# Attention in a perceiver block: the output stage one tile later, evacuations dealt out anew, input transposes between the value products

## The reference, cut to what matters

```python
# x: (32, 64, 128), ctx: (32, 128, 128), 16 heads of width 8
q = (layernorm(x) @ Wq + bq)        # 32 x 64 queries
k, v = ctx @ Wk + bk, ctx @ Wv + bv # 32 x 128 keys, values
scores = where(keep, q @ k.T / sqrt(8), neg)     # per batch row and head
out = softmax(scores) @ v
x = x + out @ Wo + bo               # stage 1, attention: the change is here
x = x + scan_block(layernorm(x))    # stage 2, a linear scan
for router in routers:              # stage 3, four layers, one expert of 16 per token
    xt = xt + w * (silu(xt @ W1[e]) @ W2[e])
```

## Time and profile before

| what | value |
|---|---|
| median of three runs | 614.9 us (609.98 to 617.53) |
| the profiled execution | 620.82 us, span of the core 619.1 us |
| TensorE busy in the span | 496.2 us (80%), granted clock 0.942 on average |
| VectorE busy | 333.5 us (54%) |
| ScalarE busy | 274.6 us (44%) |
| GpSimd busy | 197.0 us (32%) |
| chain that ended last, by engine | PE 56%, DVE 18%, issue 8%, DMA 6%, ACT 4% |

### The profile page before, as it was taken

The page is one execution under the profiler, slowest core; times in us unless marked ns, Lnnn a source line. Parts: engine busy times, 40 slices in busy tenths (PEclk is TensorE's granted clock), DMA queues, the critical chain, the costliest instruction groups (busy, mean ns, idle before and its releaser), DMA issues.

```text
span 619.1 us, 16857 instructions
## 1 busy us (share of the span) xinstructions
PE 496.2 (80%) x5788; PEld 403.8 (65%) x5788; DVE 333.5 (54%) x746; ACT 274.6 (44%) x684; POOL 197.0 (32%) x243
## 2 busy tenths in 40 slices
PE   2586868686777877799976799977799987599894
PEld 1365656575554633799943799943599963399792
DVE  3466666665664769345528445527544534744442
ACT  1455555565455430565510466620366621166440
POOL 7233131312001114433532532531541550541343
PEclk9799999998988987999999799997799997899988
DMA  5100000049200020110120110030110112010005
GB/s 134 32 17 19 12 20 12 18 150 328 81 3 2 1 68 8 35 28 19 37 85 1 39 32 15 36 94 0 31 34 9 40 42 58 22 31 19 24 31 152
DMA packets 30690, 28.11 MB, mean 45 GB/s; under 512 B 4624, under 2 KB 24464, under 8 KB 30608
## 3 DMA queue, kind: packets, MB, share of 16 engines
q1 hardware_dynamic: 26512, 18.62, 10.3%
q0 software_dynamic: 4096, 8.40, 4.4%
HBM read 20.71 MB, written 6.29 MB: 44 GB/s over the span
## 4 chain that ended last, share of the span: by engine, by line
PE 56%; DVE 18%; issue 8%; DMA 6%; ACT 4%; POOL 4%; another core or an unknown queue 1%; SPq 1%; DVEq 0%; POOLq 0%; ACTq 0%
PE bank L787 17%; PE bank L800 16%; PE bank L637 5%; DVE ppT L896 3%; PE bank L618 3%; PE bank L599 3%; DMA cur<-token_rows 3%; DVE rden L902 3%; DVE ohr L1065 2%; PE bank L593 2%; DMA ppT<-token_rows,token_i 1%; DMA token_rows<-ysort,token_i 1%; POOL token_rows L390 1%; PE bank L776 1%
## 5 line engine op out<-in xcount | busy, mean ns | idle before, releaser
L1114 DVE SCALAR_TENSOR_TENSOR pp<-pp,bank 128x512 f32<-128x512 f32 x124 | 85.4, 688 | 129.7 <-ACT pp L539 127.0
L800 PE MATMUL bank<-w,pp 128*128 x992 | 137.2, 282 | 12.7 <-DVE pp L1114 10.6
L787 PE MATMUL bank<-vm,ppT 128*128 x992 | 138.3, 285 | 0.0
L800 PEld LDWEIGHTS bank<-w,pp 128*128 128x128 f32 x992 | 123.1, 195 | 15.8 <-issue 15.3
L787 PEld LDWEIGHTS bank<-vm,ppT 128*128 128x128 f32 x992 | 126.2, 199 | 1.3 <-issue 0.2
L539 ACT ACTIVATE pp<-bank 128x512 f32<-128x512 f32 x124 | 74.2, 598 | 101.0 <-PE bank L787 87.6
L530 ACT COPY ppT<-w 128x512 f32 x124 | 75.9, 612 | 60.9 <-DVE piece_tile L1087 60.2
L390 POOL DMA_INDIRECT token_rows<-ysort,token_i x64 | 62.3, 974 | 108.1 <-DVE ysort L1124 93.0
L383 POOL DMA_INDIRECT ppT<-token_rows,token_i x64 | 61.8, 966 | 64.5 <-PE bank L776 38.4
L683 PE MATMUL bank<-trib,onesb 128*128 128x512 bf16 x308 | 78.3, 412 | 0.0
L452 ACT ACTIVATE pp<-bank,nmax 128x128 f32<-128x128 f32 x256 | 68.0, 426 | 1.9 <-DVE nmax L889 1.9
(11 more groups left out here) (182 smaller groups left out, 540.6 us busy)
## 6 DMA issues: line engine op xcount, KB each, us to landing
w<-in_L_ffn_W_dram SPq DMA_DIRECT2D x1, 4096.0 KB, 14.8
cur<-token_rows SPq DMA_DIRECT2D x16, 256.0 KB, 4.0
cx<-in_ctx_dram SPq DMA_DIRECT2D x16, 128.0 KB, 2.1
token_rows<-cur SPq DMA_DIRECT2D x1, 1024.0 KB, 5.1
ppT<-token_rows,token_i POOLq DMA_INDIRECT x64
token_rows<-ysort,token_i POOLq DMA_INDIRECT x64
out_dram<-xs SPq DMA_DIRECT2D x4, 256.0 KB, 2.7
xs<-in_x_dram SPq DMA_DIRECT2D x1, 768.0 KB, 5.7
```

The source lines that it names most:

```text
L787: last = mm(banks[2 + j % 2][:, c * P:(c + 1) * P], w1_piece[:, j % 2, c * P:(c + 1) * P], xT[:, ds(tile_of[j] * P, P)], start=True, stop= ...
L800: last = mm(banks[6 + j % 2][:, 0:D], hh[:, j % 2, c * P:(c + 1) * P], w2[:, ds(e * FF + c * P, P)], start=(c == 0), stop=(c == FC - 1))
L1114: v.scalar_tensor_tensor(hh[:, j % 2, :], th[:, j % 2, :], 1.0, banks[2 + j % 2][:, :], ALU.add, ALU.mult).then_inc(s["h_ready"], 1)
```

## The change

- **The output stage runs one tile later.** project_out(t-2) and residual(t-2) now run in tile t, and attention_out(t-2) moves to the head of VectorE's tile t, ahead of the maxima. The output projection goes to bank 7, columns 384 to 511, instead of bank 6; waits on x_updated, attn_ready and qk_evac keep it apart from the queries and keys in that bank.
- **Evacuations.** Group 2 of the transposed probabilities is copied by ScalarE at the head of its tile, and waits there for group 2's transposes; the transposed inputs are copied by VectorE, ahead of the residual. Group 2 now goes to bank 4, the inputs to bank 5.
- **TensorE's order.** scores(t), group 3 of t-1, project_qk(t+2), project_v(t+1), project_out(t-2), the 64 value products of t-1, transposes_in(t+3), the 64 sum products of t-1, groups 0, 1 and 2 of t.
- **Before and behind the loop.** VectorE copies the inputs of tiles 0, 1 and 2; the third copy stands ahead of the statistics of tiles 4 to 15 in its queue. Behind the loop the output stages of the last two tiles run. The filler products behind attention (`stay_warm`) go to bank 5.

```diff
-            def evac_inputs(t, u):
...
-                act.wait_ge(s["tr_done"], t + 1)
-                if t >= 2:
-                    act.wait_ge(s["v_done"], t - 1)
-                a.copy(aT[:, u, :], banks[4][:, 0:3 * P]).then_inc(s["a_evac"], 1)
-
             def evac_qk(t, u):
                 act.wait_ge(s["qk_done"], t + 1)
                 if t >= 2:
...
                     act.wait_ge(s["qm_ready"], t - 1)
+                    if t >= 4:
+                        act.wait_ge(s["x_updated"], t - 3)
                     for r in range(4):
                         act.wait_ge(scored[r], t - 1)
                 a.activation(qT[:, u, :], banks[7][:, 0:P], ACT.Identity, bias=bqc[:, 0:1],
...
-            def evac_pt3(t):
-                act.wait_ge(s["pt_done"], 4 * t + 4)
+            def evac_pt(t, r):
+                act.wait_ge(s["pt_done"], 4 * t + r + 1)
                 if t >= 1:
                     act.wait_ge(s["od_done"], t)
-                a.copy(ppT[:, 3, :], banks[4][:, :]).then_inc(s["pt_evac_act"], 1)
+                a.copy(ppT[:, r, :], banks[4][:, :]).then_inc(s["pt_evac_act"], 1)
 
             def tile(t, u, first, last):
-                if t + 1 < NT and not first:
+                if not first:
+                    evac_pt(t - 1, 2)
+                if not last and not first:
                     evac_qk(t + 1, 1 - u)
-                if t + 2 < NT and not first:
-                    evac_inputs(t + 2, u)
                 if not first:
-                    evac_pt3(t - 1)
+                    evac_pt(t - 1, 3)
                 for r in range(4):
                     exp_scores(t, r, first)
 
-            evac_inputs(0, 0)
             evac_qk(0, 0)
-            evac_inputs(1, 1)
             evac_qk(1, 1)
-            evac_inputs(2, 0)
             std_of(2, slice(FIRST, NT))
             each_tile(tile)
-            evac_pt3(NT - 1)
+            evac_pt(NT - 1, 2)
+            evac_pt(NT - 1, 3)
...
-                if t < 3:
-                    if t >= 1:
-                        pe.wait_ge(s["a_evac"], t)
-                else:
-                    pe.wait_ge(s["pt_evac_dve"], 3 * (t - 3) + 1)
-                nc.tensor.transpose(banks[4][:, 0:P], xln[:, u, :], ident[:])
-                nc.tensor.transpose(banks[4][:, P:2 * P], cx[:, u, 0, :], ident[:])
-                nc.tensor.transpose(banks[4][:, 2 * P:3 * P], cx[:, u, 1, :], ident[:]) \
+                if t == 1:
+                    pe.wait_ge(s["a_evac"], 1)
+                elif t >= 2:
+                    pe.wait_ge(s["v_evac"], t - 1)
+                nc.tensor.transpose(banks[5][:, 0:P], xln[:, u, :], ident[:])
...
                     .then_inc(s["tr_done"], 1)
...
             def project_qk(t, u):
                 pe.wait_ge(s["a_evac"], t + 1)
                 if t >= 1:
                     pe.wait_ge(s["qk_evac"], t)
+                if t >= 5:
+                    pe.wait_ge(s["x_updated"], t - 4)
                 mm(banks[7][:, 0:P], wq[:], aT[:, u, 0:P], start=True, stop=True)
                 mm(banks[7][:, P:3 * P], wk[:], aT[:, u, P:3 * P], start=True, stop=True) \
                     .then_inc(s["qk_done"], 1)
 
             def project_v(t, u):
-                if t >= 2:
-                    pe.wait_ge(s["pt_evac_dve"], 3 * (t - 1))
+                if t == 0:
+                    pe.wait_ge(s["a_evac"], 2)
                 elif t == 1:
-                    pe.wait_ge(s["v_evac"], 1)
+                    pe.wait_ge(s["a_evac"], 3)
+                else:
+                    pe.wait_ge(s["pt_evac_dve"], 2 * (t - 1))
                 for b in range(BT):
...
 
                 pe.wait_ge(s["exp_done"], 4 * t + r + 1)
                 if r == 3:
-                    pe.wait_ge(s["a_evac"], NT if t + 3 >= NT else t + 4)
-                elif r == 0 and (t >= 1):
-                    pe.wait_ge(s["pt_evac_act"], t)
+                    pe.wait_ge(s["pt_evac_act"], 2 * t + 1)
+                elif r == 0 and t >= 1:
+                    pe.wait_ge(s["pt_evac_act"], 2 * t)
                 elif r == 1:
-                    pe.wait_ge(s["v_evac"], NT if t + 1 >= NT else t + 2)
+                    if t + 3 < NT:
+                        pe.wait_ge(s["a_evac"], t + 4)
+                    else:
+                        pe.wait_ge(s["v_evac"], min(t + 2, NT))
                 elif r == 2:
-                    pe.wait_ge(s["pt_evac_dve"], 3 * t + 2)
-                bank = banks[4] if r in (0, 3) else banks[5]
+                    pe.wait_ge(s["pt_evac_dve"], 2 * t + 1)
+                bank = banks[5] if r == 1 else banks[4]
...
-            def values(t, u):
...
-                pe.wait_ge(s["pt_evac_dve"], 3 * t + 3)
-                pe.wait_ge(s["pt_evac_act"], t + 1)
-                pe.wait_ge(s["v_evac"], t + 1)
+            def values(t, u, which):
+
+
+                if which == 0:
+                    pe.wait_ge(s["pt_evac_dve"], 2 * t + 2)
+                    pe.wait_ge(s["pt_evac_act"], 2 * t + 2)
+                    pe.wait_ge(s["v_evac"], t + 1)
+                    if t >= 1:
+                        pe.wait_ge(s["attn_ready"], t)
+                for b in range(BT):
...
+                if which == 1:
+                    last.then_inc(s["od_done"], 1)
+
+            def project_out(t, u):
+                pe.wait_ge(s["attn_ready"], t + 1)
                 if t >= 1:
                     pe.wait_ge(s["x_updated"], t)
-                for which in range(2):
-                    for b in range(BT):
-                        for j in range(4):
-                            at = (2 * b + j // 2) * P + (j % 2) * S
-                            for r in range(4):
-                                lhsT = vm[:, t % 3, b * 4 + r, 32 * j:32 * j + 32] if which == 0 else head_ones[:, j, :]
-                                c = which * P + b * S
-                                last = mm(banks[6][32 * r:32 * r + 32, c:c + S], lhsT, ppT[:, r, at:at + S],
-                                          start=(which == 0 and b == 0 and j == 0),
-                                          stop=(which == 1 and b == 1 and j == 3))
-                last.then_inc(s["od_done"], 1)
-
-            def project_out(t, u):
-                pe.wait_ge(s["attn_ready"], t + 1)
-                mm(banks[6][:, 2 * P:3 * P], attnT[:, u, :], wo[:], start=True, stop=True) \
+                pe.wait_ge(s["qk_evac"], min(t + 4, NT))
+                mm(banks[7][:, 3 * P:4 * P], attnT[:, u, :], wo[:], start=True, stop=True) \
                     .then_inc(s["wo_done"], 1)
 
             def tile(t, u, first, last):
                 scores(t, u, first)
                 if not first:
                     transpose_probs(t - 1, 3)
+                if t + 2 < NT:
+                    project_qk(t + 2, u)
                 if not last:
                     project_v(t + 1, 1 - u)
-                if t + 2 < NT:
-                    project_qk(t + 2, u)
+                if t >= 2:
+                    project_out(t - 2, u)
                 if not first:
-                    values(t - 1, 1 - u)
-                transpose_probs(t, 0)
-                transpose_probs(t, 1)
+                    values(t - 1, 1 - u, 0)
                 if t + 3 < NT:
                     transposes_in(t + 3, 1 - u)
                 if not first:
-                    project_out(t - 1, 1 - u)
+                    values(t - 1, 1 - u, 1)
+                transpose_probs(t, 0)
+                transpose_probs(t, 1)
                 transpose_probs(t, 2)
...
             transpose_probs(NT - 1, 3)
-            values(NT - 1, 1)
+            project_out(NT - 2, 0)
+            values(NT - 1, 1, 0)
+            values(NT - 1, 1, 1)
             project_out(NT - 1, 1)
...
-            stay_warm(banks[7], 14)
+            stay_warm(banks[5], 14)
...
+            def evac_inputs(t, u):
+
+                dve.wait_ge(s["tr_done"], t + 1)
+                if t >= 2:
+                    dve.wait_ge(s["v_done"], t - 1)
+                    dve.wait_ge(s["qk_done"], t - 1)
+                v.tensor_copy(aT[:, u, :], banks[5][:, 0:3 * P]).then_inc(s["a_evac"], 1)
+
             def evac_pt(t, r):
                 dve.wait_ge(s["pt_done"], 4 * t + r + 1)
                 if t >= 1:
                     dve.wait_ge(s["od_done"], t)
-                v.tensor_copy(ppT[:, r, :], banks[4 + r % 2 if r < 2 else 5][:, :]).then_inc(s["pt_evac_dve"], 1)
+                v.tensor_copy(ppT[:, r, :], banks[4 + r][:, :]).then_inc(s["pt_evac_dve"], 1)
 
...
-                v.scalar_tensor_tensor(xt, banks[6][:, 2 * P:3 * P], keep_any[:, 0:1], xt, ALU.mult, ALU.add) \
+                v.scalar_tensor_tensor(xt, banks[7][:, 3 * P:4 * P], keep_any[:, 0:1], xt, ALU.mult, ALU.add) \
                     .then_inc(s["x_updated"], 1)
...
             def tile(t, u, first, last):
-                if not first:
-                    evac_pt(t - 1, 2)
+                if t >= 2:
```

(15 more changed lines are left out.)

10 lines of the change are left out of this document (added).

## The result

The changed kernel takes 578.0 us (median of 4 runs, 573.1 to 581.4), the kernel before 613.9 (4 runs, 610.0 to 617.5): a ratio of 0.941, 95% interval 0.932 to 0.950. The profiled execution took 581.4 us (span 579.6, mean granted clock 0.951). Its parts did not come as forecast; most of what follows is about that.

The account below looks back on a forecast made before the run. No engine was full, so the order of the work sets the time. Tiles 1 to 12 save 28.0 us, the end 3.6 and 2.7, the start loses 2.05: 32.3 off 620.82, or 582.6 off the median, range 571 to 595.

Parts of the forecast that it names:

- The relay between two tiles: Attention loop: VectorE's reciprocal, copies and residual stand between tiles by queue order alone; TensorE does small pieces for 4.94 us.
- The period: Attention loop, mask products to mask products: 7.92 us a tile instead of 10.25, bounds 7.8 and 8.1.
- The covers: Slack hiding other engines' work in each tile: 0.6 us before maxima, 0.9 for exponentials, 0.3 for VectorE's input copy, the thinnest.
- The start: Before the loop: tile 2's input copy delays the statistics, so exponentials start at 28.2 us instead of 26.14, losing 2.05.
- The table load: ScalarE before the first exponentials: 1.28 us with the next activation right behind, not the skill's added drain of about 1.38.
- One stop kept: Late in attention: TensorE's unexplained wait of 2.40 us before 150.82 us stays.
- rival 2: Same loop with more TensorE stops, a lower-clock spell and VectorE's thin cover gone: 592.4 us, chance 0.25.
- The last tiles: End of attention: tiles 13 and 14 save 3.6 us, the last tile 2.7, bounds 1.9 and 3.7.
- The sum: Whole kernel: 28.0 + 3.6 + 2.7 - 2.05 = 32.3 us off 620.82.
- Rival 4: TensorE's clock falls around its pause, with transposes alone there: 4.0 us more a tile, 667 us in all; chance 0.02.
- Transposes and the clock: End of each tile: the skill would make the last 2 us near idle; the trace shows longer such stretches do no harm.

Follow-up runs that it names:

- experiment 3: The kernel before with only attention_out, project_out and residual one tile later, on chip A: 591.6 us, ratio 0.941, period 8.17 us.
- experiment 5: The changed kernel with a second, unread reciprocal per tile ahead of VectorE's maxima, on chip B: 594.9 us, ratio 0.949.
- experiment 6: The changed kernel without the context loads of tiles 6 to 15, on chip C: 579.5 us, ratio 0.940.
- experiment 1: The changed kernel with VectorE's copy of tile 2's inputs moved behind the statistics of tiles 4 to 15, on chip A: 591.8 us, ratio 0.941.
- experiment 2: The changed kernel with the input transposes behind both halves of the products instead of between them, on chip A: 597.0 us, ratio 0.947.
- experiment 4: The changed kernel with the two 4 MB expert loads cut into 32 of 256 KB behind the context loads, on chip A: 589.4 us, ratio 0.936.
- experiment 7: The kernel before with the output stage one tile later and the expert loads in 32 pieces, on chip B: 586.3 us, ratio 0.935.
- experiment 10: The changed kernel with tile 2's input copy behind the statistics and expert loads in 32 pieces, on chip C: 568.1 us, ratio 0.924.
- experiment 8: Both kernels again on chip B, no edit: before 629.4 us, changed 592.8 us, ratio 0.945.
- experiment 9: The kernel before, unedited, run twice more on chip C: 612.8 and 612.2 us.

## Why the prediction was right, and where its parts were not

- **The mechanism held.** The relay between two tiles was queue order, and it is gone: the chain shows it, and experiment 3 shows that the output stage's move carries the whole of it. A forecast by parts would have said this only if I had costed the three edits one by one; I costed them together, and so missed that two of them pay for nothing.
- **The period: 8.18, not 7.92,** and outside the bounds of 7.8 to 8.1. Of the 0.26, input transposes are 0.13 (0.48 against 0.35; I had 0.52 as the bound and took the lower value because products ran ahead of them), the products in two pieces 0.09 (2.06 against 1.97), group 0 0.05 (0.60 against 0.55); I had also rounded 7.95 down to 7.92, and the three projections came 0.03 shorter. Half of 128 products was not half their time here: with the transposes between them each half took 1.03 us, where the whole takes 1.92 to 1.97. Over tiles 2 to 11 that is 2.6 us. The three tiles with short stops cost another 2.1.
- **The covers.** All held: 0.47 us ahead of group 0 (forecast 0.3), maxima at 1.73 (1.7), exponentials at 2.82 (2.75), input copy 0.56 (0.55), tokens over at 104.05 - 100.68 = 3.37 (3.6). What I had not seen is that behind one of them stands another (experiment 5).
- **The start.** First exponentials at 27.99, forecast 28.2. Tile 0 lost 1.63, not 2.05, but the lower clock behind the wait took up to 1.0 in tile 1. The table load: 26.69 + 1.28 = 27.97, and the next activation at 27.99. The Trainium skill (ScalarE: Activation LUTs, What ACT_TABLE_LOAD costs) adds a drain of about 1.38 us; here too the trace has no room for it.
- **One stop kept: too kind.** It took 3.15 us instead of 2.40, and more of the tile behind it ran at the lower clock. Tile 12 lost 0.64 where I had it gaining 2.33: 3.0 us. This and the short stops are rival 2 in kind, at less than its price.
- **The last tiles.** 3.55 of a possible 3.7 for the last, as its scores took 1.17 us, at full clock, and no longer 2.09; I had taken 2.7. Tiles 13 and 14 gained 3.23 of 3.6.
- **The sum.** These make 24.5 us against 32.2: by its own steps my forecast was 7.7 us too high in gain. That the total fell near it was luck, for what made up the difference was no term of mine. In later executions of the kernel before the loop loses TensorE's full clock for some tiles, and attention ends at 196.1, 201.4 and 202.4 us, while the changed kernel's ends at 168 (167.9, 167.6, and 168.2 in experiment 6 on chip C). With the ends on chip C the stage gains some 34 us, which is most of the 35.9 between the medians. On chip B the profiled pair gives 28.5, and 8 us of the medians' 36.6 show in neither of its traces. I had made the sum from a trace whose attention was the shortest of four and whose part behind it was long, 426.7 us against 408 to 410 for the same kernel on chip C. The two partly cancelled in its total, and its 5.9 us above the median told nothing of either. Rival 4 looked for a lost clock in the wrong kernel: three of the four traces of before have clean tiles at a lower clock, with 4.94 us a tile of small pieces, and in none of the seven traces of the changed loop did tiles 2 to 11 lose it.
- **Transposes and the clock.** The Trainium skill (TensorE: Matmul & The Clock Gate, Part 4: PE-mode transpose) says that transposes do not count as activity as products do. The last 2 us of a tile are transposes and a pause now, and the loop's granted clock is 1.00: by itself such a stretch does no harm here, as I had argued from the earlier trace rows.
- **What only looked like gain.** 15 of the 39.5 us between the first two spans are of the expert layers, and vanish on one chip (426.7 against 426.5). Comparing only the spans would have booked them to the change.

What is shown: the parts' sizes (experiments 1 to 4, 7), that the late stop goes with the two large loads (4, 7 and 10), the clock spells of before (8, 9). What is only argued: that the shorter relay is what keeps the changed loop's clock up behind a stop. The length of the stop alone doesn't decide, as experiment 2's 1.26 us lost nothing and before's 1.21 and 1.49 did. Open: what the short stops are, why the large loads stop TensorE, and why the loss of clock behind a stop differs.

## What to carry to other kernels

When the engines take turns, look for the steps that stand between two tiles by queue order alone and move those one tile later; then cost each further edit by itself, as experiment 3 did, for it may pay for nothing. Before a forecast, look at whether the trace of before is a typical one: its attention stage was some 9 us shorter than that of the same kernel's executions on another chip. And large loads at a full DMA share under a busy TensorE are worth cutting up: 32 pieces of 256 KB spread over the loop, in place of 2 of 4 MB, gave 5.9 us in the one tile under them, a sixth of the 35.9 us that the whole restructuring gave, for a few lines.

## What the runs showed of the hardware

- TensorE stopped for 1.9 to 3.9 us, by nothing that the profile shows, in every trace with the two 4 MB loads, and in none with the same bytes in 256 KB pieces spread over the loop.
- The same 128 products take 1.92 us in one piece (experiments 2 and 3) and 2 x 1.03 in two with three 128-column transposes between (changed kernel).
- The granted clock can stay at 1.00 through a loop with 4.94 us of relay a tile and, in another execution, fall in its middle to a mean of 0.76 over a tile, after a stop of 1.49 us (experiment 9). Behind stops of 3.15 and 3.05 us it fell to 0.50 for 5 us in the changed kernel and stayed at 1.00 in experiment 3.
- The same instructions behind attention took 408 to 414 us in the traces of chip C and 425 to 428 us in those of A and B, whichever kernel ran. Of the twelve traces on named chips, the eight on A and B have idle times of 2.5 us and more ahead of ScalarE's activation, the four on C none.
